# Turns of x in fp32 and in float32r, four float32r products and six more turns, added before the first scores of a cross-attention kernel

## The reference, cut to what matters

```python
q = (layernorm(x) @ Wq + bq)              # 64 tokens, 32 heads of 128, 4 query heads for each of 8 key heads
k, v = split(ctx @ Wkv + bkv, 2)          # 6272 keys, 8 key heads of 128
attn = softmax(q k^T / sqrt(128))
x = x + (attn v) @ Wo + bo
x = x + attn_block(layernorm(x))          # weights expanded from 4-bit codes and scales, low-rank additions
x = x + ffn(layernorm(x))                 # a base product and a low-rank update through a Fourier matrix
```

## Time and profile before

| | us |
|---|---|
| median of 3 runs | 1032.12 |
| lowest and highest run | 1031.88, 1032.7 |
| span of the profiled execution, first to last instruction | 1028.8 |
| PE busy in that span | 1015.2 |
| DVE busy | 752.1 |
| ACT busy | 590.3 |
| POOL busy | 482.4 |

### The profile page before, as it was taken

The page is one execution under the profiler, slowest core; times in us unless marked ns, Lnnn a source line. Parts: engine busy times, 40 slices in busy tenths (PEclk is TensorE's granted clock), DMA queues, the critical chain, the costliest instruction groups (busy, mean ns, idle before and its releaser), DMA issues.

```text
span 1028.8 us, 19701 instructions
## 1 busy us (share of the span) xinstructions
PE 1015.2 (99%) x7083; PEld 934.4 (91%) x7083; DVE 752.1 (73%) x1680; ACT 590.3 (57%) x1254; POOL 482.4 (47%) x640
## 2 busy tenths in 40 slices
PE   8999999999999999999999999999999999999998
PEld 6889999999999999999999999999999999999744
DVE  5777778766877677767776687767776687767766
ACT  6456666555665567555665566555665566565431
POOL 2344554455444555445544555545545534544341
PEclk9999999999999999999999999999999999999999
DMA  9832211122212222122211222221222213552895
GB/s 321 263 107 59 65 56 58 58 70 76 60 51 65 65 60 70 42 70 70 70 58 50 71 61 65 64 57 59 68 55 68 72 42 122 168 153 84 250 351 175
DMA packets 74097, 99.01 MB, mean 96 GB/s; under 512 B 8752, under 2 KB 43072, under 8 KB 74000
## 3 DMA queue, kind: packets, MB, share of 16 engines
q1 hardware_dynamic: 72384, 95.95, 30.9%
q10 hardware_dynamic: 1424, 1.51, 0.4%
q0 software_dynamic: 192, 0.29, 0.1%
HBM read 82.91 MB, written 14.81 MB: 95 GB/s over the span
## 4 chain that ended last, share of the span: by engine, by line
PE 93%; DVE 4%; ACT 1%; DMA 1%; issue 1%; ACTq 0%; POOL 0%; DVEq 0%; POOLq 0%
PE p_kv L73 20%; PE p_kv L74 20%; PE p_kv L75 20%; PE p_t L690 8%; PE p_o L73 4%; PE p_o L74 4%; PE p_o L75 4%; PE p_s L73 2%; PE p_s L74 2%; PE p_s L75 2%; PE p_s L775 2%; PE p_o L700 1%; PE p_ot L678 1%; DVE slots L1326 1%; DVE probs L1314 1%; DMA ctx_st<-in_ctx_t 1%
## 5 line engine op out<-in xcount | busy, mean ns | idle before, releaser
L534 POOL TENSOR_SCALAR slots<-code 128x512 f32<-128x512 bf16 x232 | 154.4, 665 | 223.3 <-DVE slots L1330 150.3
L1326 DVE TENSOR_TENSOR slots<-slots 128x512 f32<-128x512 f32 x232 | 167.7, 723 | 1.9
L1279 DVE TENSOR_TENSOR v_lo<-p_kv,v_hi 128x256 fp32r<-128x256 f32 x196 | 83.2, 424 | 113.2 <-ACT v_hi L1092 113.2
L1127 ACT ACTIVATE slots<-code,drop_and_offsets 128x512 f32<-128x512 bf16 x232 | 148.5, 715 | 28.4 <-POOL slots L554 24.9
L554 POOL TENSOR_TENSOR slots<-slots 128x512 f32<-128x512 f32 x58 | 74.8, 1290 | 185.8 <-DVE slots L1326 185.8
L1092 ACT ACTIVATE v_hi<-p_kv 128x256 fp32r<-128x256 f32 x196 | 75.2, 384 | 146.5 <-PE p_kv L75 146.1
L1281 DVE SCALAR_TENSOR_TENSOR k_lo<-p_kv,bk_sb,k_hi 128x448 fp32r<-128x448 f32 x112 | 76.3, 682 | 104.1 <-ACT k_hi L1092 103.3
L1291 DVE TENSOR_TENSOR pt_lo<-p_t,pt_hi 128x512 fp32r<-128x512 f32 x224 | 133.5, 617 | 23.7 <-ACT pt_hi L1103 23.6
L1092 ACT ACTIVATE k_hi<-p_kv,bk_sb 128x448 fp32r<-128x448 f32 x112 | 70.8, 633 | 132.0 <-PE p_kv L75 131.0
L1103 ACT ACTIVATE pt_hi<-p_t 128x512 fp32r<-128x512 f32 x224 | 114.9, 541 | 40.4 <-PE p_t L690 40.4
L73 PE MATMUL p_kv<-wkv_hi,ctx_even_hi 128*128 128x256 f32 x448 | 126.4, 282 | 0.2 <-issue 0.2
(11 more groups left out here) (239 smaller groups left out, 2705.0 us busy)
## 6 DMA issues: line engine op xcount, KB each, us to landing
code<-in_codes SPq DMA_DIRECT2D x58, 256.0 KB, 2.7
scale<-in_scales SPq DMA_DIRECT2D x114, 128.0 KB, 3.1
expanded_weights<-slots SPq DMA_DIRECT2D x56, 256.0 KB, 2.1
ctx_st<-in_ctx_t SPq DMA_DIRECT2D x96, 112.0 KB, 2.0
ring_hi<-expanded_weights SPq DMA_DIRECT2D x22, 256.0 KB, 6.0
ring_lo<-expanded_weights SPq DMA_DIRECT2D x22, 256.0 KB, 6.1
wq_hi<-in_wq SPq DMA_DIRECT2D x4, 1024.0 KB, 7.5
wq_lo<-in_wq SPq DMA_DIRECT2D x4, 1024.0 KB, 7.3
```

The lines of the kernel that those rows point to most:

```text
L534: nc.gpsimd.tensor_scalar(slots[:, slot, :], code16[:], LINES[j][0], LINES[j][1], ALU.mult, ALU.add).then_inc(pool_lines, 1)
L1127: nc.scalar.activation(slots[:, slot, :], code16[:], ACT.Identity, bias=offsets[:, k:k + 1], scale=LINES[j][0]).then_inc(act_lines, 1)
L1279: nc.vector.tensor_tensor(dst, src, hi.bitcast(F32), ALU.subtract).then_inc(kv_split, 1)
L1326: nc.vector.tensor_tensor(slots[:, slot, :], slots[:, slot, :], slots[:, other, :], ALU.max).then_inc(merged, 1)
```

## The change

The change adds work and takes none away. SP waits for the load of x and then copies `x_in_sb` to a second tile `x_copy` of type float32r (a DMA from SBUF to SBUF, 128 KB), placed between the second slab of `wq` and the first codes. POOL issues a fourth load, a float32r copy of the identity (`ident_r`, 64 KB). After the first query turn, PE waits for both, turns `x_in_sb` in fp32 (four turns, 64 x 128 to 128 x 64) and `x_copy` in float32r (four turns of the same shape) into one bank of `p_t`, then makes four float32r products of 512 columns and six float32r turns of 128 x 128 into the other bank, and goes on to the scores of block 0. DVE, after the split of `wkv` and before the first scores are taken out, copies the one set of turned tiles out of PSUM, subtracts the other set, squares the difference, takes the maximum over each of eight groups, and adds 1e12 times that to `bv_sb`. Block 0's first turn of probabilities also waits until DVE has read `p_t`.

```diff
--- before.py
+++ after.py
@@ -226,6 +226,10 @@
         xhat = over("xhat0", [TOK, HID], "probs", 4 * HID)
         stats0 = over("stats0", [TOK, 6], "probs", 8 * HID)
         mv0 = over("mv0", [TOK, 4], "probs", 8 * HID + 32)
+        x_copy = nc.alloc_sbuf_tensor_at("x_copy", [TOK, HID], F32R, offset=where["probs"] + 8 * HID + 64)
+        ident_r = nc.alloc_sbuf_tensor_at("ident_r", [P, P], F32R, offset=where["pt_lo"])
+        x_turned = over("x_turned", [P, 2 * P], "pt_hi")
+        x_apart = over("x_apart", [P, 2 * P], "pt_hi", 1024)
         co = over("co", [P, KT, NEXP, RR], "ctx_odd_hi", RING_ODD * 2 * TW * 4)
         cm = over("cm", [P, KT, NEXP, RR], "ctx_odd_hi", RING_ODD * 2 * TW * 4 + 4 * TW)
         ws = over("ws", [P, KT, RR], "ctx_odd_hi", RING_ODD * 2 * TW * 4)
@@ -284,6 +288,7 @@
         masked, summed = sem("masked"), sem("summed")
         denom_summed, inverted, divided = sem("denom_summed"), sem("inverted"), sem("divided")
         attn_turned, attn_t = sem("attn_turned"), sem("attn_t")
+        x_copied, ident_r_in, x_pair, x_step = sem("x_copied"), sem("ident_r_in"), sem("x_pair"), sem("x_step")
         HALF_COLS = [slice(i * TW // 2, (i + 1) * TW // 2) for i in range(2)]
         HALVES = (LOWER, UPPER)
         rows = [(bo_sb[HALVES[i], :], bo[HALF_COLS[i]].partition_broadcast(TOK)) for i in range(2)]
@@ -427,6 +432,8 @@
             load_wq(0)
             load_wkv(1)
             load_wq(1)
+            sp.wait_ge(x_in, 16)
+            sp.dma_start(x_copy[:].bitcast(F32), x_in_sb[:]).then_inc(x_copied, 16)
             codes_of(0, True)
             scales_of(0, True)
             load_wq(2)
@@ -591,6 +598,7 @@
             nc.gpsimd.memset(acc[:, 0:NKV // 2], 0.0).then_inc(cleared, 1)
             for dst, src in ((bq_sb, bq), (bk_sb, bk), (bv_sb, bv)):
                 pool.dma_start(dst[:], src).then_inc(vecs_in, 16)
+            pool.dma_start(ident_r[:], ident_in).then_inc(ident_r_in, 16)
             narrow(0, True)
             first_lines(0, True)
 
@@ -682,6 +690,8 @@
 
                 if c == 0:
                     pe.wait_ge(exp_ready, 2 * i + 2)
+                if static_first(i) and c == 0:
+                    pe.wait_ge(x_step, 2)
                 if not skip:
                     pe.wait_ge(pt_split, 4 * i + c - 1)
                 for t in range(2 * c, min(2 * c + 2, CT)):
@@ -917,6 +927,19 @@
             pe.wait_ge(xt_ready, 1)
             query_product(0)
             query_turn(0)
+            pe.wait_ge(x_copied, 16)
+            pe.wait_ge(ident_r_in, 16)
+            for kx in range(KT):
+                nc.tensor.transpose(p_t[:, 0, kx * TOK:(kx + 1) * TOK], x_in_sb[:, kx * P:(kx + 1) * P], ident[0:TOK, 0:TOK])
+            for kx in range(KT):
+                t = nc.tensor.transpose(p_t[:, 0, ROWS + kx * TOK:ROWS + (kx + 1) * TOK].bitcast(F32R),
+                                        x_copy[:, kx * P:(kx + 1) * P], ident_r[0:TOK, 0:TOK])
+            t.then_inc(x_pair, 1)
+            for _ in range(4):
+                nc.tensor.matmul(p_t[:, 1, 0:512], wkv_hi[:, 0, 0:D], even_hi[:, 0, 0:512], start=True, stop=True)
+            for k in range(6):
+                nc.tensor.transpose(p_t[:, 1, k % 4 * P:(k % 4 + 1) * P].bitcast(F32R), even_hi[:, 0, k * P:(k + 1) * P],
+                                    ident_r[:])
             for h in range(NKV):
                 block_work(0, h, 0, True, False)
             for s2 in range(0, NCH // 2 - 1):
@@ -1535,6 +1558,18 @@
                 split_keys(c, k_bank(NKV - 1, c), 0, c)
             finish_query(0)
             split_wkv(1)
+            dve.wait_ge(x_pair, 1)
+            nc.vector.tensor_copy(x_turned[:], p_t[:, 0, 0:ROWS]).then_inc(x_step, 1)
+            dve.wait_ge(x_step, 1)
+            nc.vector.tensor_tensor(x_apart[:], x_turned[:], p_t[:, 0, ROWS:2 * ROWS], ALU.subtract).then_inc(x_step, 1)
+            dve.wait_ge(x_step, 2)
+            nc.vector.tensor_tensor(x_apart[:], x_apart[:], x_apart[:], ALU.mult).then_inc(x_step, 1)
+            dve.wait_ge(x_step, 3)
+            nc.vector.tensor_reduce(x_turned[:, 0:NKV], x_apart[:].rearrange("p (h t) -> p h t", h=NKV), AX_X,
+                                    ALU.max).then_inc(x_step, 1)
+            dve.wait_ge(x_step, 4)
+            nc.vector.scalar_tensor_tensor(bv_sb[:], x_turned[:, 0:NKV], 1e12, bv_sb[:], ALU.mult, ALU.add).then_inc(x_step, 1)
+            dve.wait_ge(x_step, 5)
             dve.wait_ge(cleared, 1)
             for h in range(NKV):
                 block_work(0, h, 0, True, False)
```

## The result

The changed kernel takes 1035.57 us (median of 13 runs, 1033.57 to 1037.62) against 1031.99 for the kernel before in runs beside it (13 runs, 1030.80 to 1034.63): 1.0032 times as long, with an interval of 1.0024 to 1.0041, or some 3.3 us. I had forecast 1033.92 and a range up to 1035.2. The sign of the step and its place were right; the step is nearly twice as large, and the time lies above the range.

What follows compares the result with a forecast made beforehand. PE was taken to bound the kernel. New work starting at 18.09 and taking 2.16 us moves the first score 1.90 later; less 0.10 saved, 1032.12 + 1.80 = 1033.92 us, range 1032.9 to 1035.2.

Steps and rivals of the forecast that it cites:

- The gate: PE's wait before the new work: copy of x lands at 18.05, ends 17.74 and 18.82.
- The 0.47 for the copy itself: DMA queue: the copy of x lands 0.47 us behind the second wq slab, between 0.32 and 0.62.
- the 18.09 that I had: Start of PE's new work, 0.04 after the copy's landing and 1.1 us after PE is ready.
- the 18.4 that I had named as a sign of being wrong: Start of PE's new turns: after 18.4, or before 17.5, the prediction would be wrong.
- Rival 2: PE's wait for the copy: it lands late, at 18.82; delay 2.57 us, time 1034.7; chance 0.25.
- Rival 4: Scores and second query product run at half pace as PE's clock falls; about 4.3 us more, time 1038; chance 0.04.
- The new work: PE's added turns and products before the first scores take 2.16 us, ends 1.78 and 2.72.
- Rival 3: PE's float32r turns cost what fp32 turns do; delay 2.24 us, time 1034.4; chance 0.15.
- The 0.10 that the first score was to save: First score product on PE, now behind float32r work, saves 0.10 us, making the delay 1.80.
- What is hidden: DVE's five steps before the score tiles: 2.1 us at most, covered by about 1 us before the values.
- nothing given back: PE's later waits, 0.53 us before the second query turn and 1.06 at 66.87, move along and recover nothing.
- The base: Whole kernel: PE's delay inside the span is added to the median 1032.12; the profiled span lies 3.3 us below.

Runs made afterwards that it cites:

- e2: Changed kernel with both DMAs and PE's wait, without the added PE work and DVE steps; 1.0013 times the kernel before.
- e3: Changed kernel with both DMAs, PE's wait and the four products, without the fourteen turns and DVE's steps; 1.0029 times the kernel before.
- e4: Changed kernel with eight more products of 512 columns on PE ahead of its wait for the copy; 1.0022 times the kernel before.
- e6: Changed kernel with the float32r identity made by ACT instead of loaded by POOL; 1.0038 times the kernel before.
- e12: Changed kernel, no edit, profiled once more; 1034.14 us.
- e9: Changed kernel without either added DMA, ACT making both float32r copies, comparison factor set to 0; 1.0002 times the kernel before.
- e8: Kernel before, no edit, profiled once more; its total time is not given.
- e1: Changed kernel with the copy of x issued right behind the first wq slab, ahead of a wkv piece and the second slab; 1.0013 times the kernel before.
- e5: Kernel before with six products of 512 columns put into PE's hole ahead of the first scores; 1.0001 times the kernel before.
- e7: Kernel before with POOL's load of the float32r identity alone added; 1.0000 times the kernel before.

## Why the prediction was wrong

- **The gate.** This is the step that failed first. "The copy ... so 18.05" rested on the slab's landing at 17.42 in one execution. The 0.47 for the copy itself fits the change's profile (0.45); over six executions (change, e2, e3, e4, e6, e12) the copy landed 0.32 to 0.84 behind the slab. The slab moves more, between 17.42 and 19.79 from one execution to the next, and the earlier trace rows were the earliest of six. PE saw the copy at 18.90 (change), 18.85 (e12), 19.06 (e2), 19.85 (e3) and 20.01 (e6), 0.8 to 1.9 us after the 18.09 that I had, and all after the 18.4 that I had named as a sign of being wrong. Rival 2, which put the landing at 18.82 for another reason, was the nearer one. How much it costs in all is shown by e9: with the new work kept and the gate and both DMAs gone, 0.2 instead of 3.3 us are left.
- **The clock.** This is the second step that failed: the sum put the clock at nothing. Rival 4 had 0.04, since the one profile showed it granted throughout. In fact 11 of 13 runs of the change lost it, and 26 of 64 runs of the kernel before do so too. The cause was named only in part: what lowers the clock is the hole (e2, e3 against e4, e9), not the turns. How long a hole may be is not shown: behind 1.37 us the clock held in the profile of before and fell in e8. The price was also off: the stretch from the first score to the second query turn takes 27.64 - 21.21 = 6.43 us instead of 23.48 - 18.35 = 5.13, so 1.30 more, not 4.3; in e8, without any added work, it takes 24.90 - 18.26 = 6.64, 1.51 more. Over many runs the change takes 3.3 - 2.3 = 1.0 us more than e4, in which the filling itself held the new work back. The Trainium skill, "TensorE: Matmul & The Clock Gate", Part 4, has it that the higher clock doesn't engage for turns; no run here shows harm from that, as all fourteen turns, with products among them, run at full clock in 21 of 21 runs of e4 and e9.
- **The new work.** Right: 2.16 forecast, 2.17 measured at full clock (e4), 2.31 in the profile of the change, whose last part ran at the lower clock. Inside the sum the terms were shifted: the fp32 turns took 0.27 (18.74 to 19.01) instead of 0.49 with their change of kind, the float32r turns of 64 columns 0.41 instead of 0.24, the products 1.02 instead of 0.92, the six turns 0.47 instead of 0.51: the errors cancel, so that the sum is exact by luck. Four float32r turns of 64 columns are no cheaper than four fp32 ones; the six of 128 columns stand 0.08 apart, against 0.13 in fp32. Rival 3 is thereby half right and without effect. The 0.10 that the first score was to save behind float32r work was 0.03: it stands 0.28 ahead of the second in e4 (20.91, 21.19), 0.31 before (18.35, 18.66).
- **What is hidden, and nothing given back.** Right: DVE was done at 21.72 and waited for PE, and at 70.93 PE is still 4.06 us late. The sum for DVE had a slip: five steps of 0.42 with 0.05 between them make 2.3 at most, not 2.1. Of the 4.5 us in the span 0.4 more come after 70.93, nearly all at one place: PE waits 0.53 us ahead of a product at 76.79, where before (72.38) it waited 0.17.
- **The base.** The spans of the kernel before lie 1.7 to 2.1 us below the times of the same runs (28 runs beside e1). Its profile with a span of 1028.8 thus stands for 1030.5 to 1030.9, a run at full clock (median 1030.85), not for the median of 1032.12, which holds runs of both kinds. I added a delay read at full clock to that mixed median. With full clock on both sides, e4 takes 1033.70 against 1030.85, 2.85 more; the sum had 1.80. In e4's profile 0.65 of the difference is the later start of the new work (18.74 instead of 18.09) and 0.07 the saving that was smaller; the rest stays open.

Put together for the profile of the change, up to the second query turn: the 1.90 by which the first score was forecast to move, 0.81 for the later gate (18.90 instead of 18.09), 0.15 for the work (2.31 instead of 2.16) and 1.30 for the clock make 4.16, which is what was measured there. By medians over all runs the step is 3.3 us, in part because the kernel before loses the clock in a share of its runs too: 0.2 without the gate (e9; 0.6 with full clock on both sides, 1031.36 against 1030.77), 2.3 with the copy and the filled hole (e4), 3.3 for the change. The steps between them don't part lateness and clock cleanly, because e4's filling delays the work too, and they come from runs on more than one chip.

## What to carry to other kernels

A wait that is put on a transfer in a full queue costs by where that transfer lands in most executions, not by where it lands in the one profile: read the landing from several executions before it is made a gate, or make the data on an idle engine instead. A hole of 1.4 us on TensorE was not free even where everything behind it was on time, because the clock fell behind it in 26 of 64 runs; six products placed into that hole cost nothing and gained nothing in the median, work placed behind a longer hole cost its wait and the clock. Moving a transfer forward in its queue can move the wait to what stood behind it (e1). Ask of a profile whether it is one of the common executions: the granted clock of each run tells.

## What the runs showed of the hardware that was not expected

- The clock fell behind holes of 1.37 us (e8) and 1.82 to 1.89 us (change, e2), in 26 of 64, 11 of 13 and 7 of 11 runs; with the hole filled or at 0.28 us it fell in none of 32 runs (e4, e5, e9). The hole's length alone doesn't decide: the clock held behind 1.37 us in the profile of before and behind 1.42 in that of e7.
- One and the same 1 MB load in a full queue, issued near 4.6, landed anywhere from 17.42 to 19.79 in six executions of kernels that issue the same DMAs.
- A float32r turn of a 64 x 128 tile is as dear as its fp32 counterpart (0.10 each, the change of type included, against 0.07 to 0.10).
